# Macaron block on 8 cores: eight tiles of x on one queue, seven places for layer norm, constant products wherever no attention runs

## What is computed

```python
x = x + 0.5 * ffn(_layernorm(x))
x = x + attn(_layernorm(x))
x = x + 0.5 * ffn(_layernorm(x))

def ffn(xf):
    cluster_scores = xf @ cluster_sigs.T          # 8 clusters
    tile_scores = xf @ sigs.T                     # 64 tiles, ternary signatures
    tile_idx = cluster_idx * TPC + local_idx      # argmax of calibrated gates, twice
    h = gelu(xf @ compress_w1 + compress_b1)      # 256 wide
    comp = tanh(h @ compress_w2 + compress_b2)    # 2 wide
    hh = relu(einsum('ni,nig->ng', comp, spline_w1[tile_idx]) + spline_b1[tile_idx])
    mag = einsum('ng,ngo->no', hh, spline_w2[tile_idx]) + spline_b2[tile_idx]
    return layernorm(xf + mag * directions[tile_idx] * output_scale) * gamma + beta

def attn(x):   # 16 query heads of 64, 4 key and value heads, causal, 2048 positions
    out = softmax(mask(q @ k.T / 8)) @ v
    return layernorm(out) @ Wo + bo
```

## Time and profile before

| | us |
|---|---|
| median of 3 runs | 618.8 (618.64 to 619.91) |
| the profiled execution, whole | 622.25 |
| its span on the slowest core (core 0) | 620.7 |
| spans of the other cores | 610.4 to 618.5 |
| PE busy on core 0 | 480.4 (77%) |
| ACT busy | 410.1 (66%) |
| DVE busy | 383.1 (62%) |
| first logits on PE | 99.11 |
| last product of the last attention | about 566.3 |

### The profile page before, as it was taken

One profiled execution on the slowest core, in us unless ns is written; L12 is line 12 of the kernel. 1 busy time (PEld: TensorE's weight loads), 2 busy tenths in 40 slices (PEclk: granted clock), 3 DMA queues, 4 the chain that ended last, 5 costly groups with the idle time before them and its releaser, 6 DMA issues.

```text
span 620.7 us, 14753 instructions; the slowest of 8 cores (610.4 to 620.7 us)
## 1 busy us (share of the span) xinstructions
PE 480.4 (77%) x5187; PEld 286.1 (46%) x5229; DVE 383.1 (62%) x1134; ACT 410.1 (66%) x458; POOL 98.8 (16%) x187
## 2 busy tenths in 40 slices
PE   0438799777987599967998778889989988785742
PEld 0326455543544345644564334445555555453331
DVE  4656876877678346583443562647877683847564
ACT  1667756978338957778779763758886794995320
POOL 1211103432021211131112210110110110011100
PEclk9977999968989669999999888979999998989866
DMA  8979200223101210003008000040170133022011
GB/s 201 214 129 236 86 2 10 61 60 78 35 10 27 53 42 11 18 10 79 16 5 154 11 19 1 14 81 14 42 195 11 23 145 75 18 75 115 1 69 68
DMA packets 66908, 39.00 MB, mean 63 GB/s; under 512 B 59776, under 2 KB 61952, under 8 KB 66708
## 3 DMA queue, kind: packets, MB, share of 16 engines
q1 hardware_dynamic: 63460, 30.19, 18.9%
q0 software_dynamic: 2800, 5.77, 5.8%
q10 hardware_dynamic: 576, 2.10, 1.3%
HBM read 21.27 MB, written 8.39 MB: 48 GB/s over the span
## 4 chain that ended last, share of the span: by engine, by line
PE 48%; DVE 13%; ACT 12%; issue 11%; DMA 9%; POOL 2%; SPq 2%; DVEq 1%; ACTq 0%; POOLq 0%
PE pALL L99 47%; ACT sE L241 7%; DMA sX<-x 5%; DMA sT<-sXN 3%; DVE sX L209 2%; ACT sXN L241 2%; DVE sST L233 2%; ACT L241 2%; SPq L105 2%; POOL sE L1044 1%; PE pTR L197 1%; ACT sHT L241 1%; DVE sAN L205 1%; POOL sRS L205 1%; DVE sXN L201 1%
## 5 line engine op out<-in xcount | busy, mean ns | idle before, releaser
L241 ACT ACTIVATE sE<-pALL,sNB 128x1024 bf16<-128x1024 f32 (+1 forms) x288 | 288.3, 1066 | 105.3 <-PE pALL L99 91.8
L99 PE MATMUL pALL<-sVTM,sE 128*128 128x65 bf16 x2176 | 110.7, 199 | 15.9 <-POOL sE L1044 14.8
L99 PE MATMUL pALL<-sQT,sKT 64*128 64x256 bf16 (+1 forms) x1152 | 103.7, 278 | 24.3 <-ACT sE L241 22.5
L99 PEld LDWEIGHTS pALL<-sVTM,sE 128*128 128x128 bf16 x2176 | 90.2, 101 | 63.4 <-issue 50.4
L1044 POOL TENSOR_SCALAR_AFFINE_SELECT sE<-sE 128x256 bf16<-128x256 bf16 x128 | 55.1, 431 | 319.5 <-ACT sE L241 311.2
L209 DVE SCALAR_TENSOR_TENSOR sX<-pALL,sRS,sX 128x512 f32<-128x512 f32 x96 | 70.9, 745 | 29.7 <-PE pALL L99 28.5
L99 PE MATMUL pALL<-sWQ,sT 128*128 128x512 bf16 x237 | 64.6, 405 | 13.2 <-DMA sT<-sAN 4.0
L99 PEld LDWEIGHTS pALL<-sQT,sKT 64*128 64x128 bf16 x1152 | 40.5, 95 | 49.8 <-issue 38.1
L99 PE MATMUL pALL<-sT,sWQ 128*128 128x512 bf16 x244 | 57.7, 380 | 2.6 <-issue 1.3
L241 ACT ACTIVATE sXN<-sX,sNM,sRS 128x1024 bf16<-128x1024 f32 x30 | 36.8, 1236 | 21.3 <-DVE sNM L209 11.6
L233 DVE BATCH_NORM_STATS2 sST<-sX 128x6 f32<-128x512 f32 x68 | 44.3, 676 | 3.8 <-DMA sX<-x 3.8
(11 more groups left out here) (174 smaller groups left out, 574.2 us busy)
## 6 DMA issues: line engine op xcount, KB each, us to landing
y<-sX SPq DMA_DIRECT2D x16, 512.0 KB, 2.7
sX<-x SPq DMA_DIRECT2D x12, 512.0 KB, 14.9
sX<-x ACTq DMA_DIRECT2D x4, 512.0 KB, 9.3
sWQ<-wq POOLq DMA_DIRECT2D x2, 1024.0 KB, 21.3
sWQ<-wo POOLq DMA_DIRECT2D x1, 2048.0 KB, 14.1
sT<-sAN SPq DMA_TRANSPOSE x39, 2.4
sSG<-sd SPq DMA_DIRECT2D x1, 512.0 KB, 11.0
sW1C<-cw POOLq DMA_DIRECT2D x1, 512.0 KB, 11.7
```

Of the source, the lines that this page charges most:

```text
L99: return self.op("t", lambda e: e.matmul(out, lhsT, rhs, start=start, stop=stop, **kw), *after, ns=self.array(n))
L241: return lambda e: e.activation(*a, **k)
```

## The change

Three parts.

1. Loads: ACT issues tiles 0 to 7 of x at the start. POOL's Wk now waits for tile 5, its first half of Wq for tile 7, the second half for the first; SP's tiles 8 to 11 wait for tile 7, tiles 12 to 15 for Wv. The planned landing times are other numbers.
2. Places: `xn_ring` has seven places at first, the three of `sXN` and the four of `sE`. Before the first attention it goes back to three, and the first exponentials wait for the turns that read the `sE` places.
3. Constant products: allowed wherever `first` is None, so also between attentions and after the last one.

```diff
-        if groups[0] == 0 and now > 32e3 and soonest - now > 100.0 and P.low() and hum():
+        if first is None and now > 32e3 and soonest - now > 100.0 and P.low() and hum():
...
-    for t, at in enumerate((6.5e3, 9.7e3, 13.5e3, 18e3)):
+    for t, at in enumerate((6.7e3, 9.7e3, 13.5e3, 18e3, 22e3, 24.5e3, 27e3, 29.5e3)):
         load_x("s", t, at)
...
-        yield "g", xt[2]
-        W["k"] = load("g", "Lwk", sWK, d_wk, 29.5e3, xt[3])
-        for t in range(4, 8):
-            load_x("y", t, 23.5e3 + 2.3e3 * t, xt[3])
+        yield "g", xt[5]
+        W["k"] = load("g", "Lwk", sWK, d_wk, 35e3, xt[5])
+        for t in range(8, 12):
+            load_x("y", t, 37e3 + 4.5e3 * (t - 8), xt[7])
+        yield "g", xt[7]
+        W["q"] = [load("g", "Lwq0", sWQ[:, :, 0:512], d_wq[:, :, 0:512], 49e3, xt[7])]
+        yield "g", W["q"][0]
+        W["q"].append(load("g", "Lwq1", sWQ[:, :, 512:1024], d_wq[:, :, 512:1024], 65e3, W["q"][0]))
         yield "g", None
-        W["q"] = [load("g", "Lwq0", sWQ[:, :, 0:512], d_wq[:, :, 0:512], 41e3)]
-        yield "g", xt[7]
-        W["q"].append(load("g", "Lwq1", sWQ[:, :, 512:1024], d_wq[:, :, 512:1024], 64.5e3, xt[7]))
-        yield "g", None
-        W["v"] = load("g", "Lwv", sWV, d_wv, 67e3)
-        for t in range(8, NT):
-            load_x("y", t, 24e3 + 2.5e3 * t, xt[7] if t < 12 else xt[t - 4])
+        W["v"] = load("g", "Lwv", sWV, d_wv, 70e3)
+        for t in range(12, NT):
+            load_x("y", t, 74e3 + 2.5e3 * (t - 12), W["v"])
...
-    xn_ring = Banks(range(3))
+    xn_ring = Banks(range(7))
+
+    def xn(i):
+        return sXN[:, i] if i < 3 else sE[:, i - 3].rearrange("p h q -> p (h q)")
...
-    weave(P, None, others, 0.0, lambda: fring.held <= {6, 7}, count, hum)
+    xn_ring.slots = [0, 1, 2]
+    weave(P, None, others, 0.0, lambda: fring.held <= {6, 7} and xn_ring.held <= {0, 1, 2}, count, hum)
+    e_free[:] = [xn_ring.free[3 + j] for j in range(4)]
```

More of the change, by code:

```diff
@@ L482, in load @@
         return tok
-    for t, at in enumerate((6.5e3, 9.7e3, 13.5e3, 18e3)):
+    for t, at in enumerate((6.7e3, 9.7e3, 13.5e3, 18e3, 22e3, 24.5e3, 27e3, 29.5e3)):
         load_x("s", t, at)
-    tidb = load("y", "Lidb", sIDB[:], d_idb, 6.2e3)
-    tc = load("y", "Lc", sCST[:], d_cst, 8.2e3)
-    tsg = load("y", "Lsg", sSG[:], d_sd, 13e3)
+    tidb = load("y", "Lidb", sIDB[:], d_idb, 6.9e3)
+    tc = load("y", "Lc", sCST[:], d_cst, 9.8e3)
+    tsg = load("y", "Lsg", sSG[:], d_sd, 14.5e3)
     td68 = load("y", "Ld68", sD68[:], d_d68, 20e3)
@@ L491, in build_program @@
     tg68 = load("y", "Lg68", sG68[:], d_g68, 23e3)
-    tsel = load("y", "Lsel", sSEL[:], d_sel, 24.5e3)
-    tidf = load("y", "Lidf", sIDF[:], d_idf[:, 0:20], 24.5e3)
-    tl6 = load("y", "Ll6", sL6[:], d_l6, 24.6e3)
-    tbvb = load("y", "Lbvb", sBVB[:], d_bvb, 23e3)
-    tlnb = load("y", "Llnb", sLNB[:], d_lnb, 23e3)
-    tmsk = load("y", "Lmsk", sMSK[:], d_msk, 23e3)
+    tsel = load("y", "Lsel", sSEL[:], d_sel, 27e3)
+    tidf = load("y", "Lidf", sIDF[:], d_idf[:, 0:20], 29.5e3)
+    tl6 = load("y", "Ll6", sL6[:], d_l6, 31e3)
+    tbvb = load("y", "Lbvb", sBVB[:], d_bvb, 34e3)
+    tlnb = load("y", "Llnb", sLNB[:], d_lnb, 35e3)
+    tmsk = load("y", "Lmsk", sMSK[:], d_msk, 36e3)
     tcw1 = load("g", "Lcw1", sW1C[:], d_cw1, 18e3, xt[0])
@@ L502, in th_loads @@
     def th_loads():
[L504 to L517 removed]
+        yield "g", xt[5]
[6 more added lines that the diff above has]
+        W["q"].append(load("g", "Lwq1", sWQ[:, :, 512:1024], d_wq[:, :, 512:1024], 65e3, W["q"][0]))
+        yield "g", None
+        W["v"] = load("g", "Lwv", sWV, d_wv, 70e3)
+        for t in range(12, NT):
+            load_x("y", t, 74e3 + 2.5e3 * (t - 12), W["v"])
+    P.clock.update(s=5e3, y=6e3, g=9e3)
     def cst(c, n=1):
@@ L634, in ln_block @@
                 if key[0] == "a":
-                    x = op("s", I.activation(sXN[:, i, :], sX[:, t, :], AF.Copy, accum_out=sSU[:, t, 0:1]), ready[t], fr, ns=1150)
+                    x = op("s", I.activation(xn(i), sX[:, t, :], AF.Copy, accum_out=sSU[:, t, 0:1]), ready[t], fr, ns=1150)
                     yield "v", x
@@ L641, in ln_block @@
                 yield "s", a
-                q = op("s", I.activation(sXN[:, i, :], sX[:, t, :], AF.Square, bias=sMV[:, t, 0:1], accum_out=sSQ[:, t:t + 1]), a, x, fr, ns=1150)
+                q = op("s", I.activation(xn(i), sX[:, t, :], AF.Square, bias=sMV[:, t, 0:1], accum_out=sSQ[:, t:t + 1]), a, x, fr, ns=1150)
                 yield "v", q
@@ L668, in ln_block @@
             if early:
-                n = op("s", I.activation(sXN[:, i, :], sX[:, t, :], AF.Identity, bias=sNM[:, t:t + 1], scale=sRS[:, t:t + 1]), a, fr, ns=1150)
+                n = op("s", I.activation(xn(i), sX[:, t, :], AF.Identity, bias=sNM[:, t:t + 1], scale=sRS[:, t:t + 1]), a, fr, ns=1150)
                 f, bank, fr = yield from bank_for(n, tidb)
                 for c in range(NC):
-                    m = op("t", I.transpose(pTR[:, bank, c, :], sXN[:, i, 128 * c:128 * (c + 1)], sIDB[:]), n, tidb, fr, ns=110)
+                    m = op("t", I.transpose(pTR[:, bank, c, :], xn(i)[:, 128 * c:128 * (c + 1)], sIDB[:]), n, tidb, fr, ns=110)
                 if t < 4 or key[0] == "c" and t % 2:
@@ L682, in ln_block @@
                 if slow:
-                    n = op("s", I.activation(sXN[:, i, :], sX[:, t, :], AF.Identity, bias=sNM[:, t:t + 1], scale=sRS[:, t:t + 1]), a, fr, ns=1150)
+                    n = op("s", I.activation(xn(i), sX[:, t, :], AF.Identity, bias=sNM[:, t:t + 1], scale=sRS[:, t:t + 1]), a, fr, ns=1150)
                 else:
-                    n = v(I.tensor_scalar(sXN[:, i, :], sX[:, t, :], sRS[:, t:t + 1], sNM[:, t:t + 1], ALU.mult, ALU.add), a, fr, ns=650)
-                d = P.dma("y", f"TX{i}", sT[:, :, 128 * t:128 * (t + 1)], sXN[:, i, :], n, transpose=True)
+                    n = v(I.tensor_scalar(xn(i), sX[:, t, :], sRS[:, t:t + 1], sNM[:, t:t + 1], ALU.mult, ALU.add), a, fr, ns=650)
+                d = P.dma("y", f"TX{i}", sT[:, :, 128 * t:128 * (t + 1)], xn(i), n, transpose=True)
                 xn_ring.give(i, d)
```

1 line of the change is left out of this document (removed).

## The result

The changed kernel took 622.71 us (median of 9 executions), the kernel before 618.64 beside it (9 executions). One of the nine with the change ran in a slower state of the chip (641.36 us) and stands outside the ratio. That is 1.0090, with a 95% interval of 1.0058 to 1.0122: the change is slower by 0.9% (the two medians are 4.1 us apart), where 615.0 was forecast.

A forecast was written before the change was run, and what follows sets the result against it. PE's work paces the middle; chains through transfers, ACT and DVE bound start and end. Profiled 622.25 - 1.3 (start) + 1.5 (middle) - 4.0 (end) = 618.45; from the median, 618.8 - 3.8 = 615.0 us, range 609.5 to 621.5.

The forecast's parts named there:

- The sum's -1.3: Start: first logits 1.3 us earlier through the new loads, with ends from 5 us earlier to 2 us later.
- That execution is 3.45 us above the median of 618.8, so: 618.8 - 3.8: Whole kernel: step from the profiled execution, 622.25 us and forecast at 618.45, to a forecast median of 615.0 us.
- the walk: Start: step-by-step times through first front, chain and layer norm; last sNM at 73.1 us, not 73.73, last turn 2 us earlier.
- The charge: Middle: 4,104 more columns between first and last logits cost 1.9 us, charged 1.5; new order 3 us either way.
- Rival (b): Middle: the new order loses 3 us more and the end wins as said; 618 us, chance 0.10.
- -4.0 forecast: End, behind the last attention: 4.0 us shorter, between 5.5 (clock full throughout) and 1 (it falls anyway).
- stay at 1.00: End: 27 constant products keep PE's granted clock at 1.00 from the last attention until wo.
- rival (d): End: clock at half, 39 constant products take 8.8 us in a 5.98 us gap, 2.8 late; 619.5 us, chance 0.08.
- The limit of 13/16: PE clock: skill's current limit with three cores busy; by it the end would win some 0.5 us less.
- The signs that were named: Right if: gelu 40.5 to 41.5, tile 7 before 32.5, logits 96 to 99, clock near 1.00, wo 0.24, end 4 us shorter.
- rival (a): Start: the loads pay in full, first logits 5 us earlier; with the end about 611 us, chance 0.15.
- the signs against: Wrong if: DVE idle over 1 us at tile 4's sNM, constants running when sOHP is ready, middle over 3 us longer.

The follow-up runs named there:

- e1: Kernel before with the third part alone, constant products allowed wherever no attention runs; loads and places of before: 613.46 us, ratio 0.9924 to before.
- e6: The kernel of e1 with the planner's clock of PE put 0.1 us later ahead of the first attention: 618.21 us, ratio 0.9974 to before.
- e7: The kernel of e1 with the planner's clock of PE put 0.1 us later ahead of the fourth attention only: 628.03 us, ratio 1.0130 to before.
- e8: The kernel of e1 with the planner's clock of PE put 0.3 us later ahead of the first attention: 614.15 us, ratio 0.9911 to before.
- e9: The kernel of e1 with the seven places for layer norm's intermediates added, loads of before: 615.20 us, ratio 0.9944 to before.
- e4: The changed kernel without its third part, constant products only ahead of the first logits as before: 630.32 us, ratio 1.0212 to before.

## Why the prediction was wrong

**The start: right for the core that was read, wrong for the kernel.** The sum's -1.3 is -1.4 from core 0 to the slowest core after. But core 0's start was the longest of eight. The wait of 4.56 us for tile 4 is that core's: core 2 had its first sum of tile 4 at 30.65 us, straight behind the exponential, its one-hot at 40.84 and its first logits at 92.52. For the mean core the change costs 3.0 against the 95.3 of that execution, 3.6 against the mean of the six traces with before's loads and start (before, e1, e6 to e9: 94.7). Two steps failed here. The first turned the profiled execution into the forecast: "That execution is 3.45 us above the median of 618.8, so: 618.8 - 3.8". That takes a gain read on the latest core for a gain on every core, and on five of the eight no such wait was there to be won (their gelu came at 37.4 to 38.9 us, core 0's at 42.23). How much of the 3.45 was core 0's late start isn't shown: four of the five other traces also have a core at 98.5 to 100.7. The second is in "I take 1.3 us for the first logits": the walk ends at the last turn and carries its gain through to the logits, with nothing put for the stretch behind the first key product, which the new order makes 3.0 us longer under either set of loads: 3.0 of the 3.6. Which of its rows cost how much (PE's wait of 1.17 us, the later `sNMX`, the copy of `sWT`) is read from the traces and was not tried one by one. The walk itself had its errors, which nearly cancelled: the exponential was put at 35 us and came at 32.57, the gelu at 40.7 to 41.5 and came at 38.03, the one-hot at 45.5 and came at 43.03; what followed to the first logits took 54.7 us, not 52.3.

**The middle: mis-sized.** The charge was 1.5 us, for 4,104 columns, with 3 either way for the order; it is 4.1 on the mean core (4.3 against the mean of the five kernels with before's order, 463.3). The columns' price wasn't what failed; the order's was put at nothing in the sum. A list of a few hundred pieces re-drawn by 0.1 us of planned time moves the middle from 462.3 to 473.9, 2.1 us of it columns, with all but the last attention untouched (e7). Rival (b), "nothing in the rows binds the planner's times to the chip's", was the right one and had 0.10. Its 3 us are about what this draw cost (2.6 to 2.8 beyond the charge), but under a third of what e7's cost.

**The end: right.** -4.0 forecast, -3.9 measured (mean), and -4.2 from e1 with constants alone and before's columns. Within it one thing was wrong: the clock did not stay at 1.00 in the slowest core (0.68 from 572 to 576 us, with PE busy for 2.42 of the 4 us before). On six of the eight cores it reads 0.50 in one of the first two stretches of 2 us behind the last attention; from 6 us behind it on, all eight read 1.00 again. On the slowest core 19 constants took 3.86 us, and the `sMS` turn stood 0.35 us behind its data. That is rival (d), worth a few tenths. `wo`'s products were 0.24 us each as said. The limit of 13/16 that the Trainium skill gives (TensorE: Matmul & The Clock Gate, "Part 1: The HAM clock gate") doesn't show there: by it they would have taken 0.29, an estimate (16/13 of 0.24). The row that the prediction holds against it, 1.00 from 250 to 350 us, is core 0's alone; the other seven read 0.93 to 0.98 there, all above 13/16 (0.81), and are made up of stretches at 1.00 and at 0.50 only. The two savings of the end, the constants' 4.2 and the 5,384 columns' 2.2 (e4's 53.5 against 55.7), don't add to 6.4; the changed kernel has 3.9. The fall of the clock on six cores, which e1 has on none, is a part of it; the rest is not settled.

**The signs that were named.** Tile 7 landed before 32.5 us (SP's next issue, which waits for it, is at 28.82), first logits at 97.70 between 96 and 99, `wo` at 0.24, an end shorter by 4 us: these came, and rival (a)'s earlier first logits did not. Two did not come as named: the gelu was earlier than 40.5 to 41.5 (38.03), and the clock was not near 1.00 throughout. So most signs for the forecast came and the forecast was wrong: they were signs for its start and end on the core that was read. Of the signs against, one fired, "a middle longer by over 3 us".

**The sum on the mean core:** +3.6 start, +4.3 middle, -3.9 end: +4.0 us, where the forecast had -1.3, +1.5 and -4.0. So the start is 4.9 us of the miss, the middle 2.8, the end 0.1, together 7.8, where forecast and measurement are 7.7 apart. The timed executions give +5.4 for the mean core (617.4 against 612.0). The last 1.4 us are not attributed; traces of kernels with the same start lie up to 2.4 us apart at the first logits (93.8 to 96.2).
